# New places for all stages of a software-pipelined kernel, and the bias products moved to its prologue

## The chip, the cores and the metric

One core of a Trainium2 chip. The time is the device time of one execution, in microseconds (us). PE is TensorE, DVE VectorE, ACT ScalarE, POOL GpSimd, SP the engine that issues the transfers here.

## The reference, cut to what matters

x is 8 x 16 x 16 tokens of 64 channels. First comes a deformable convolution, then a mixture of experts of which two of eight are kept per token:

```python
xn = layernorm(x)                                    # over the channels
x_proj = xn @ w_in + b_in
x1 = gelu(layernorm(depthwise_conv3x3(xn)) * gamma + beta)
offset = x1 @ w_off + b_off                          # 8 groups x 9 taps x 2
mask = softmax(x1 @ w_mask + b_mask)                 # over the 9 taps
out = sum over taps of mask * bilinear_sample(x_proj, position + offset)
x = x + out @ w_out + b_out
z = layernorm(x)
w = the two largest of softmax(z @ Wr + br), divided by their sum
h_e = gelu((z * ln_g[e] + ln_b[e]) @ W1[e] + b1[e])
x = x + sum over e of w_e * (h_e @ W2[e] + b2[e])
```

ln_b[e] @ W1[e] + b1[e] does not depend on the tokens. The kernel computes it once, as eight products of 64 x 8 by 64 x 256 that add up in one PSUM bank (bias_product, line 1612), and puts it as two extra rows, high and low part, under the experts' first weights (bias_rows, line 925).

## The kernel before

The 2048 tokens are four chunks of 512 (CHUNKS), each of four tiles of 128. The program of every engine is a prologue, four bodies (j = 0 to 3) and a tail. Body j does three things side by side:

- The sampling of chunk j, in 36 steps (NP: four group pairs of nine taps). A step makes interpolation weights by two products (weights_t), ACT brings them to SBUF (weights_out), and a step and a half later PE multiplies them with the image (gather: 4 tiles x 3 products). Six tile results fill one of two PSUM banks; DVE multiplies a full bank with the column weights (weigh, 24 times a body). PE may start bank m only when bank m - 2 was weighed. After nine steps POOL adds the taps (tap_tree) and DVE adds the lanes in two halves (lane_sum).
- The preparation of chunk j + 1 ("a"): transposes of the normalised input (input_t), its low part (input_low), convolution (convolve, four), projection, the image's transposes (image_t, image_out), LayerNorm and Gelu (conv_norm, conv_t, conv_gelu), offsets, and on DVE positions, clamps, cells, rows, fractions, products (the last parts of the features), edges, hats, tap weights and column weights; features_t and table_out make the table for the steps of the next body.
- The experts for chunk j - 1 ("d"): samples_t, project_out, residual, inner_norm, experts_t, zn_low, router, route, 16 expert_in, 16 hidden (Gelu on ACT), four expert_out of two experts, outputs_out, outputs_t, outputs_in and, on POOL, combine.

In body 3 there is no next chunk. Its chunk is done in two halves of two tiles, so that it has 72 places with half as much work each, the experts for chunk 2 run beside it, and the experts of its own first half are begun (half_samples_t and the others). The tail does the experts of chunk 3.

What sets the order is a table for each engine and body (PE_FIRST to POOL_LAST, from line 62): for every stage the place at which the engine's program issues it. Places run from 0 to 35.5 in halves (0 to 71.5 in body 3). At a whole place n stands weights_t of step n, at n + 0.5 the gather of step n - 1; weighing m is issued at the place where its last step ends, after the stages of the same place. A place is an order within one engine's program, no time: where a stage waits for another engine, the engine's program stands at that place.

Products of zeros (keep_clock, line 1622) keep PE busy in waits; FILL holds their numbers in the prologue, "zeros" the places in bodies 0 and 3 where two are made. SP (line 500) loads all inputs, then waits for the two bias rows (line 521) and copies them with 16 transfers of 16 x 16 values into the weights' rows; PE waits for these before body 1 (line 1823).

## Time and profile before

| | |
|---|---|
| three executions | 310.0, 309.98, 307.35 us |
| median | 309.98 us |
| the profiled execution's own time | 309.92 us |
| its span, first to last instruction | 308.1 us |
| PE busy | 269.5 us (87%) |
| DVE busy | 238.4 us (77%) |
| ACT busy | 190.3 us (62%) |
| POOL busy | 120.6 us (39%) |
| mean clock granted to PE | 0.972 of 2.4 GHz |

A busy time counts a PE product with its way through the pipeline, so products that follow each other overlap; their cost is the distance of two starts. The windows further down divide the span by bodies: body 0 begins at 31.3 us with the first product of its step 0, body 1 at 89.2, body 2 at 158.2, body 3 at 222.5, and the last gather ends at 282.6.

### The profile page before, as it was taken

The page shows a single profiled execution, that of the slowest core. Times are in us where ns is not written, and L with a number is a line of the kernel's source. Part 1 is how long each engine was busy: PE and PEld are TensorE (multiplying, and loading weights), DVE is VectorE, ACT ScalarE, POOL GpSimd, SP SyncE. Part 2 cuts the span into 40 slices and gives each one's busy share as a digit, 9 for nine tenths or more (in the row PEclk, how much of TensorE's full clock was granted, in tenths as well). Part 3 has the DMA queues.
Part 4 walks back from the last instruction along what each step waited for, and adds up shares of the span by engine and source line. Part 5 has one row for each costly group of instructions (what it writes and reads, how often), then busy time and mean ns, then how long its engine had stood idle before and what let it go on. Part 6 is the DMA issues. An engine that isn't in the chain of part 4 may idle for free.

```text
span 308.1 us, 8247 instructions
## 1 busy us (share of the span) xinstructions
PE 269.5 (87%) x3312; PEld 178.5 (58%) x3312; DVE 238.4 (77%) x680; ACT 190.3 (62%) x351; POOL 120.6 (39%) x123
## 2 busy tenths in 40 slices
PE   6975999774897998899799999988978999989795
PEld 2552467542565766354477765535757788677462
DVE  6999868999977589995889589998757446189455
ACT  3786446573753397788365678775545685746363
POOL 6230132310750431405096605050575373648530
PEclk9998999999897899999999999997999999999999
DMA  5920000000000000000000000000000000000000
GB/s 149 291 54 0 2 3 3 3 0 0 2 2 0 2 4 3 2 0 2 0 2 20 2 3 0 2 0 2 3 17 2 2 3 2 9 2 2 10 2 17
DMA packets 7187, 4.83 MB, mean 16 GB/s; under 512 B 5089, under 2 KB 6830, under 8 KB 7086
## 3 DMA queue, kind: packets, MB, share of 16 engines
q1 hardware_dynamic: 7150, 4.31, 5.7%
q8 instruction: 26, 0.43, 0.6%
q14 instruction: 11, 0.09, 0.1%
HBM read 2.04 MB, written 0.52 MB: 8 GB/s over the span
## 4 chain that ended last, share of the span: by engine, by line
PE 43%; DVE 39%; POOL 10%; issue 4%; ACT 2%; DMA 1%; DVEq 0%; POOLq 0%; ACTq 0%
DVE prod L891 6%; DVE samp L906 4%; PE ga_ps L1579 4%; PE z_ps L1547 3%; PE z_ps L1549 3%; PE ga_ps L1581 3%; PE m_ps L1681 3%; PE ga_ps L1580 3%; PE z_ps L1561 3%; POOL prod L566 2%; PE m_ps L1648 2%; PE m_ps L1693 2%; PE m_ps L1664 2%; PE m_ps L1650 2%; PE m_ps L1471 2%
## 5 line engine op out<-in xcount | busy, mean ns | idle before, releaser
L1306 ACT ACTIVATE wk<-z_ps 128x512 int32<-128x512 f32 x108 | 64.6, 598 | 56.4 <-PE z_ps L1549 55.9
L1579 PE MATMUL ga_ps<-v_all,wk 128*128 128x80 f16 x576 | 79.3, 204 | 11.4 <-DVE prod L891 11.1
L891 DVE TENSOR_TENSOR prod<-ga_ps,wx 128x480 f32<-128x480 f32 x96 | 61.6, 650 | 27.6 <-PE ga_ps L1581 27.3
L566 POOL TENSOR_TENSOR prod<-prod 128x960 f32<-128x960 f32 (+1 forms) x20 | 36.5, 1825 | 113.5 <-DVE prod L891 113.5
L1579 PEld LDWEIGHTS ga_ps<-v_all,wk 128*128 128x128 f16 x576 | 57.7, 101 | 38.4 <-issue 17.3
L1580 PE MATMUL ga_ps<-v_all,wk 128*128 128x80 f16 x576 | 79.2, 204 | 0.0
L1581 PE MATMUL ga_ps<-v_all,wk 128*128 128x80 f16 x576 | 79.1, 204 | 0.0
L1580 PEld LDWEIGHTS ga_ps<-v_all,wk 128*128 128x128 f16 x576 | 58.2, 101 | 7.9 <-issue 1.1
L1581 PEld LDWEIGHTS ga_ps<-v_all,wk 128*128 128x128 f16 x576 | 58.4, 101 | 0.0
L1547 PE MATMUL z_ps<-tab,sel_hi 128*128 128x512 f16 x108 | 42.6, 394 | 0.5 <-ACT tab L1298 0.5
L1549 PE MATMUL z_ps<-tab,sel_lo 128*128 128x512 f16 x108 | 42.4, 393 | 0.0
L1337 ACT ACTIVATE h_all<-m_ps 128x512 f32<-128x512 f32 x64 | 36.9, 601 | 7.3 <-PE m_ps L1650 6.3
L1313 ACT ACTIVATE wk<-z_ps 128x512 int32<-128x512 f32 x36 | 21.5, 597 | 19.8 <-PE z_ps L1561 19.8
L906 DVE TENSOR_REDUCE samp<-prod 128x16 f32<-128x320 f32 x48 | 20.5, 476 | 2.4 <-POOL prod L568 1.8
L568 POOL TENSOR_TENSOR prod<-prod 128x320 f32<-128x320 f32 (+1 forms) x20 | 17.8, 892 | 1.6
L1561 PE MATMUL z_ps<-tab,sel_hi 128*128 128x256 f16 x72 | 17.7, 273 | 0.2 <-ACT tab L1298 0.2
L1561 PE MATMUL z_ps<-tab,sel_lo 128*128 128x256 f16 x72 | 17.6, 272 | 0.0
L1625 PE MATMUL ga_ps<-still 128*128 128x512 f16 x52 | 14.9, 428 | 3.0 <-DVE uloc L807 1.2
L567 POOL TENSOR_TENSOR prod<-prod 128x320 f32<-128x320 f32 (+1 forms) x20 | 15.6, 781 | 1.6
L1648 PE MATMUL m_ps<-zn_both,w_high 128*128 128x256 f16 x64 | 15.7, 274 | 0.2 <-ACT h_all L1337 0.2
L1650 PE MATMUL m_ps<-zn_high,w_low 97*128 97x256 f16 x64 | 15.7, 273 | 0.0
L1664 PE MATMUL m_ps<-h_all,w_s 128*64 128x512 f32 x64 | 15.5, 605 | 0.0
(279 smaller groups left out, 577.0 us busy)
## 6 DMA issues: line engine op xcount, KB each, us to landing
v_all<-still SPq DMA_DIRECT2D x1, 1440.0 KB, 10.7
h_all<-in_W SPq DMA_DIRECT2D x1, 512.0 KB
w_s<-in_W SPq DMA_DIRECT2D x1, 512.0 KB
x_tok<-in_x SPq DMA_DIRECT2D x1, 384.0 KB, 6.7
out_dram<-x_tok SPq DMA_DIRECT2D x6, 64.0 KB, 1.7
w_high<-w_high SPq DMA_DIRECT2D x1, 256.0 KB, 3.0
const<-in_table SPq DMA_DIRECT2D x1, 218.0 KB, 2.7
vec<-in_vectors SPq DMA_DIRECT2D x1, 132.5 KB
```

The lines of the kernel that those rows point to most:

```text
L566: then(pool.tensor_tensor(p[:, 0:3, :], p[:, 0:3, :], p[:, 3:6, :], ALU.add))
L891: dve.tensor_tensor(prod[q % 2][:].rearrange("p k n -> p (k n)")[:, f * PB * NV:(f + 1) * PB * NV] .rearrange("p (n c l) -> p n c l", n=PB ...
L906: ins = dve.tensor_reduce(samp[:, t, 2 * q:2 * q + 2, :], prod[q % 2][:, 5:K2, t * NV:(t + 1) * NV] .rearrange("p k (c g l) -> p g c k l", ...
L1306: act.activation(wk[n % WR][:], z_ps[use % 2][:], ACT.Relu, scale=HIGH_UNIT * FINE / Z_UNIT).then_inc(s_wk, 1)
L1337: act.activation(h_t[n % HR].rearrange("p a n -> p (a n)"), m_ps[n % 2], ACT.Gelu, scale=1.0 / (W1_SCALE * Z_SCALE)).then_inc(s_ht, 1)
L1547: pe.matmul(z_ps[use % 2][:], sel_hi[:, 2 * k:2 * k + 2, :].rearrange("p g m -> p (g m)"), tab[j % 2][:, q, :], start=True, stop=False)
L1549: pe.matmul(z_ps[use % 2][:], sel_lo[:, 2 * k:2 * k + 2, :].rearrange("p g m -> p (g m)"), tab[j % 2][:, q, :], start=False, stop=True).th ...
L1561: ins = pe.matmul(to, sel[:, 2 * k:2 * k + 2, :].rearrange("p g m -> p (g m)"), tab[LAST % 2][:, q, tokens_of(half)], start=(sel is sel_hi ...
L1579: pe.matmul(to, w_h, high, start=True, stop=False)
L1580: pe.matmul(to, w_h, low, start=False, stop=False)
L1581: ins = pe.matmul(to, w_l, step, start=False, stop=True)
L1648: pe.matmul(m_ps[n % 2][:, a * 2 * P:(a + 1) * 2 * P], w1_high[:, c0:c0 + P], zn_both[:, i * 2 * P:(i + 1) * 2 * P], start=True, stop=False)
```

## The change

All tables get new places. The stages of the preparation go some 2 to 12 places later in bodies 0 to 2, the expert stages some 5 to 10 places later; in body 3 the expert stages of chunk 2 go from places 11 to 48 to places 32 to 71.5, and those of the first half from 50 to 60.5 to 69 to 71.5. Two lines of the tables and what they became, of PE in body 1 and of DVE in body 0:

```diff
-PE_SECOND = {"input_t": 0, "convolve": [5, 5.5, 6, 10], "project": 4, "image_t": [11, 12], "conv_t": 14, "offsets": 15.5,
+PE_SECOND = {"input_t": 2.5, "convolve": [13.5, 15.5, 7, 7.5], "project": 12, "image_t": [17, 18.5], "conv_t": 22.5,
...
-             "zn_low": 17, "route": [18, 23, 25.5], "expert_weights": 26, "b2": 0, "bias_rows": 5, "router_parts": 31,
+             "zn_low": 17, "route": [18, 23, 25.5], "expert_weights": 26, "b2": 2.5, "bias_rows": 27, "router_parts": 8,
```

The eight bias products leave body 0 of PE (places 0 to 5.5). Four stand in the prologue after the convolutions, where FILL[3] goes from 13 products of zeros to 3, and four after the offsets, where FILL[4] goes from 7 to 0. They write the second gather bank instead of the second m bank; ACT copies the result to SBUF, DVE's bias_rows reads that copy, and PE's second gather bank waits for it once.

```diff
@@ -134,7 +132,7 @@
 
 
 
-FILL = [9, 2, 9, 13, 7, 6, 2]
+FILL = [9, 2, 9, 3, 0, 6, 2]
 
 FIRST = -(-6 * TP // PB)
 HALF_FIRST = -(-6 * TH // PB)
@@ -255,6 +253,7 @@
         b2_col = sb("b2_col", [P, E // 2])
         b1_in = sb("b1_in", [E, HID])
         b1_sum = sb("b1_sum", [E, HID])
+        lnb_w1 = sb("lnb_w1", [E, HID])
         b1_high = sb("b1_high", [E, HID], F16)
         b1_low = sb("b1_low", [E, HID], F16)
         lng_s = sb("lng_s", [C, E])
@@ -427,6 +426,7 @@
         s_still = sem("s_still")
         s_lngs = sem("s_lngs")
         s_lnb_ps = sem("s_lnb_ps")
+        s_lnb = sem("s_lnb")
         s_bias = sem("s_bias")
         s_w1h = sem("s_w1h")
         s_w1d = sem("s_w1d")
@@ -924,8 +924,9 @@
 
             def bias_rows():
 
-                dve.wait_ge(s_lnb_ps, 1)
-                link(dve.tensor_tensor(b1_sum[:], m_ps[1][0:E, 0:HID], b1_in[:], ALU.add))
+                dve.wait_ge(s_lnb, 1)
+                dve.wait_ge(s_wd, N_WD)
+                link(dve.tensor_tensor(b1_sum[:], lnb_w1[:], b1_in[:], ALU.add))
                 ins = dve.tensor_scalar(b1_high[:], b1_sum[:], W1_SCALE, None, ALU.mult)
                 ins.then_inc(s_bias, 1)
                 dve.wait_ge(s_bias, 1)
@@ -1337,6 +1338,11 @@
                 act.activation(h_t[n % HR].rearrange("p a n -> p (a n)"), m_ps[n % 2], ACT.Gelu,
                                scale=1.0 / (W1_SCALE * Z_SCALE)).then_inc(s_ht, 1)
 
+            def bias_product_out():
+
+                act.wait_ge(s_lnb_ps, 1)
+                act.copy(lnb_w1[:], ga_ps[1][0:E, 0:HID]).then_inc(s_lnb, 1)
+
             def high_w1():
 
                 act.wait_ge(s_wd, N_WD)
@@ -1444,6 +1450,7 @@
             ins.then_inc(s_sel, 1)
             for l in range(LOC):
                 distance(0, l)
+            bias_product_out()
             table_out(0, 0)
             tap_exp(0)
             table_out(0, 1)
@@ -1569,6 +1576,8 @@
                 for i, t in enumerate(tiles):
                     slot = n * len(tiles) + i
                     m, at = slot // PB, slot % PB
+                    if at == 0 and FILLS * j + m == 1:
+                        pe.wait_ge(s_lnb, 1)
                     if at == 0 and FILLS * j + m >= 2:
                         pe.wait_ge(s_ga_rd, FILLS * j + m - 1)
                     high, low, step = (v[:, 2 * j + t // 2, part, q, :, :, :].rearrange("p c g l -> p (c g l)")
@@ -1613,8 +1622,7 @@
 
                 if e == 0:
                     pe.wait_ge(s_wd, N_WD)
-                    pe.wait_ge(s_vd, 1)
-                ins = pe.matmul(m_ps[1][0:E, 0:HID], lnb_at(e), w1_raw[:, e * HID:(e + 1) * HID],
+                ins = pe.matmul(ga_ps[1][0:E, 0:HID], lnb_at(e), w1_raw[:, e * HID:(e + 1) * HID],
                                 start=(e == 0), stop=(e == E - 1))
                 if e == E - 1:
                     ins.then_inc(s_lnb_ps, 1)
@@ -1748,13 +1756,10 @@
                     if j == 0:
                         for at_zeros in at["zeros"]:
                             if n == at_zeros:
-                                pe.wait_ge(s_bias, 2)
+                                pe.wait_ge(s_vd, 1)
                                 keep_clock(m_ps[1], 2)
                         if n == at["b2"]:
                             columns_b2()
-                        for e in range(E):
-                            if n == at["bias_product"][e]:
-                                bias_product(e)
                     if has_a:
                         if n == at["input_t"]:
                             input_t(j + 1)
@@ -1802,12 +1807,16 @@
             for t in range(TP):
                 convolve(0, t)
             keep_clock(ga_ps[0][:], FILL[3])
+            for e in range(E // 2):
+                bias_product(e)
             pe.wait_ge(s_ident, 2)
             image_t(0, 0)
             conv_t(0)
             image_t(0, 1)
             pe.wait_ge(s_ones, 1)
             offsets(0)
+            for e in range(E // 2, E):
+                bias_product(e)
             keep_clock(ga_ps[0][:], FILL[4])
             pe.wait_ge(s_uloc, 1)
             keep_clock(ga_ps[0][:], FILL[5])

```

On PE, in the prologue, behind the last convolution (still is the tile of zeros, h_all holds the raw first weights, vec the experts' LayerNorm biases), before:

```order
L1493 MATMUL m_ps<-bias,ones 128x64
L1625 MATMUL ga_ps<-still 128x512 x13
L1514 MATMUL m_ps<-own_row,xq_left 64x96
L1515 MATMUL m_ps<-row_below,xq_left 64x32
L1514 MATMUL m_ps<-own_row,xq_left 64x96
```

and now:

```order
L1500 MATMUL m_ps<-bias,ones 128x64
L1633 MATMUL ga_ps<-still 128x512 x3
L1625 MATMUL ga_ps<-h_all,vec 8x256 x4
L1521 MATMUL m_ps<-own_row,xq_left 64x96
L1522 MATMUL m_ps<-row_below,xq_left 64x32
```

Four bias products stand between the remaining zeros and the image's transposes.

On DVE, in body 0, around the bias rows (b_sum, b_high, b_low; prod<-ga_ps is a weighing, samp<-prod a lane sum), before:

```order
L891 TENSOR_TENSOR prod<-ga_ps,wx 128x480
L928 TENSOR_TENSOR b_sum<-m_ps,b_in 8x256
L929 TENSOR_SCALAR b_high<-b_sum 8x256
L932 SCALAR_TENSOR_TENSOR b_low<-b_sum,b_high 8x256
L891 TENSOR_TENSOR prod<-ga_ps,wx 128x480
L740 SCALAR_TENSOR_TENSOR xq<-m_ps,image_bias,xq 64x256 x2
L744 COPY xq_left<-xq 128x2x16x3
L891 TENSOR_TENSOR prod<-ga_ps,wx 128x480 x2
L906 TENSOR_REDUCE samp<-prod 128x16 x4
L942 SCALAR_TENSOR_TENSOR w_low<-h_all,lng_s,w_high 64x256 x2
L891 TENSOR_TENSOR prod<-ga_ps,wx 128x480
```

and now, with the parts of the features that follow them (feat, fine, low, wf, shape, low_at, rest):

```order
L891 TENSOR_TENSOR prod<-ga_ps,wx 128x480 x2
L929 TENSOR_TENSOR b_sum<-lnb_w,b_in 8x256
L930 TENSOR_SCALAR b_high<-b_sum 8x256
L933 SCALAR_TENSOR_TENSOR b_low<-b_sum,b_high 8x256
L820 TENSOR_SCALAR feat<-frq 128x16x18
L822 SCALAR_TENSOR_TENSOR fine<-feat 128x288
L823 SCALAR_TENSOR_TENSOR low<-fr,feat 128x288
L825 SCALAR_TENSOR_TENSOR wf<-feat,fine 128x288
L891 TENSOR_TENSOR prod<-ga_ps,wx 128x480 x2
L830 TENSOR_SCALAR feat<-low 128x16x18
L831 TENSOR_TENSOR shape<-wf,csq 128x288
L833 SCALAR_TENSOR_TENSOR low_at<-feat 128x288
```

The three instructions moved from behind the third weighing to behind the eighteenth.

On PE, near the end of body 3, behind the transposes of the first half's normalised tokens (const,zn; the router is w_r_high and w_r_low, h_all,w_s an expert's second product, const,y_sb the outputs' transposes, ga_ps<-v_all,wk the gather, z_ps<-tab the weights of a step), before:

```order
L1469 MATMUL m_ps<-const,zn 64x128 x2
L1561 MATMUL z_ps<-tab,sel_hi 128x256
L1561 MATMUL z_ps<-tab,sel_lo 128x256
L1561 MATMUL z_ps<-tab,sel_hi 128x256
L1561 MATMUL z_ps<-tab,sel_lo 128x256
L1579 MATMUL ga_ps<-v_all,wk 128x80
L1580 MATMUL ga_ps<-v_all,wk 128x80
L1581 MATMUL ga_ps<-v_all,wk 128x80
L1579 MATMUL ga_ps<-v_all,wk 128x80
L1580 MATMUL ga_ps<-v_all,wk 128x80
L1581 MATMUL ga_ps<-v_all,wk 128x80
```

and now, where it is the last place of the body:

```order
L1588 MATMUL ga_ps<-v_all,wk 128x80
L1589 MATMUL ga_ps<-v_all,wk 128x80
L1590 MATMUL ga_ps<-v_all,wk 128x80
L1476 MATMUL m_ps<-const,zn 64x128 x2
L1613 MATMUL m_ps<-w_r_high,zn_both 128x8
L1614 MATMUL m_ps<-w_r_low,zn_both 128x8
L1613 MATMUL m_ps<-w_r_high,zn_both 128x8
L1614 MATMUL m_ps<-w_r_low,zn_both 128x8
L1689 MATMUL m_ps<-h_all,w_s 64x256 x8
L1701 MATMUL m_ps<-const,y_sb 128x128 x8
L1588 MATMUL ga_ps<-v_all,wk 128x80
L1589 MATMUL ga_ps<-v_all,wk 128x80
```

The router followed six steps after its transposes and now follows at once, and behind it stand the last expert products, the outputs' transposes and the last gathers.

## Rows read from the trace of the kernel before

**Rows 1.** Windows: busy time by engine; bodies 0 to 3.

```profile
31.30:89.20 57.90, 48.06 (x665) 30.56 (x664) 51.33 (x138) 32.41 (x55) 17.18 (x13) 0.97 0.01 2
89.20:158.20 69.00, 62.40 (x764) 39.58 (x762) 54.09 (x147) 45.24 (x80) 23.90 (x18) 0.95 0.01 2
158.20:222.50 64.30, 60.73 (x760) 38.71 (x758) 55.59 (x138) 43.75 (x79) 25.55 (x23) 0.97 0.02 4
222.50:282.60 60.10, 55.27 (x774) 45.03 (x775) 36.57 (x95) 35.11 (x67) 35.31 (x37) 1.00 0.02 5
```

**Rows 2.** Waits by engine, longest first.

```profile
PE z_ps L1539 <- DVE feat L843: 7.0, 2, 4.1
...
DVE prod L891 <- PE ga_ps L1581: 27.3, 23, 3.0
```

**Rows 3.** Timeline of PE: first product of two steps in a row.

```profile
52.02 0.38 PE L1547 MATMUL z_ps<-tab,sel_hi 128*128 128x512 f16 x1
...
52.88 0.38 PE L1547 MATMUL z_ps<-tab,sel_hi 128*128 128x512 f16 x1
```

**Rows 4.** Windows: start of body 0, places 3 to 6 of body 1, 70 to 80.

```profile
31.30:46.20 14.90, 14.90 (x195) 8.29 (x194) 11.32 (x31) 6.78 (x13) 3.91 (x3) 1.00 0.01 3
92.30:103.40 11.10, 9.01 (x99) 6.70 (x96) 6.42 (x22) 3.55 (x7) 2.50 (x2) 0.69 0.01 1
...
70.00:80.00 10.00, 5.25 (x55) 3.44 (x53) 8.95 (x24) 4.41 (x8) 1.49 (x1) 0.83 0.01 2
```

**Rows 5.** Timeline of PE: a bias product (two passes a row).

```profile
40.76 0.60 PE L1617 MATMUL m_ps<-h_all,vec 64*8 64x256 f32 x2
```

**Rows 6.** Timeline of PE and ACT in the prologue.

```profile
12.16 2.97 PE L1625 MATMUL ga_ps<-still 128*128 128x512 f16 x13
...
15.42 0.24 PE L1514 MATMUL m_ps<-own_row,xq_left 128*64 128x96 f16 x2 [0.29 <-DVE xq_left L744]
...
22.33 1.47 PE L1625 MATMUL ga_ps<-still 128*128 128x512 f16 x6 [1.17 <-DVE uloc L807]
...
12.79 3.30 ACT L1345 ACTIVATE w_high<-h_all,lng_s 64x256 f16<-64x256 f32 x8 [0.48 <-DMA b_in<-in_b]
```

**Rows 7.** Timeline of DVE and SP, and landings of b1's rows.

```profile
42.16 0.41 DVE L932 SCALAR_TENSOR_TENSOR b_low<-b_sum,b_high 8x256 f16<-8x256 f32 x1
...
48.25 5.76 SPq L524 DMA_DIRECT2D w_low<-b_low  x8
...
DMA to landing us min/median/max: 1.7/1.7/2.9
```

**Rows 8.** Timeline of DVE in body 0: stages counted behind the bias rows.

```profile
69.98 0.29 DVE L820 TENSOR_SCALAR feat<-frq 128x288 f16<-128x288 f32 x1
71.53 0.31 DVE L830 TENSOR_SCALAR feat<-low 128x288 f16<-128x288 f32 x1
74.54 0.65 DVE L891 TENSOR_TENSOR prod<-ga_ps,wx 128x480 f32<-128x480 f32 x1
76.22 0.45 DVE L862 TENSOR_REDUCE esum<-ex 128x32 f32<-128x288 f32 x1
77.78 0.65 DVE L891 TENSOR_TENSOR prod<-ga_ps,wx 128x480 f32<-128x480 f32 x1
```

**Rows 9.** The chain of waits, in order of time: a pair of experts out.

```profile
131.95 1.87 PE m_ps L1664 x8
```

**Rows 10.** Timeline of PE and ACT, end of body 3: transposes, router, copies.

```profile
274.43 0.38 PE L1469 MATMUL m_ps<-const,zn 128*64 128x128 f32 x2
...
276.51 0.18 PE L1604 MATMUL m_ps<-w_r_high,zn_both 128*128 128x8 f16 x1
...
266.80 1.56 ACT L1365 ACTIVATE y_sb<-m_ps,b_col 128x256 f32<-128x256 f32 x4
```

**Rows 11.** One line's instructions (ns min/median/max), and POOL beside the slow one.

```profile
L781 DVE TENSOR_SCALAR pyc<-py x4: 300/640/1317, 20.4 to 186.4; 128x288 f32<-128x288 f32 x4
...
58.72 2.22 POOL L566 TENSOR_TENSOR prod<-prod 128x960 f32<-128x960 f32 x1 [5.43 <-DVE prod L891]
```

More of the change, by code:

```diff
@@ L58 @@
 TINY = 2.0 ** -120
-PE_FIRST = {"input_t": 4, "convolve": [7, 8.5, 8.5, 9.5], "project": 6.5, "image_t": [10, 11.5], "conv_t": 14.5, "offsets":
-            15.5, "table": [24.5, 27], "samples_t": 24.5, "project_out": 8.5, "experts_t": 17.5, "router": 27, "expert_in":
-            [22, 35.5, 35.5, 35.5, 35.5, 35.5, 35.5, 35.5, 35.5, 35.5, 35.5, 35.5, 35.5, 35.5, 35.5, 35.5], "expert_out":
-            [17, 17.5, 20.5, 21, 21, 22.5, 25, 30], "outputs_t": [29.5, 30], "b2": 0, "bias_product": [0, 0, 1, 1, 3, 4, 4.5,
-            5.5], "zeros": [19, 22, 18.5]}
@@ L96 @@
-DVE_THIRD = {"input_stats": 0, "input_norm": 19.5, "input_low": 0, "conv_stats": 10, "project_low": 4.5, "conv_norm": 10,
-             "image_out": 12.5, "positions": [13.5, 14.5, 14], "rows": [18, 18, 19.5, 24], "edges": 18.5, "hats": 30,
-             "tap_weights": [29, 31], "lane_sum": [13, 17.5, 21, 23, 27.5, 29, 0, 0], "residual": 3, "inner_norm": 5,
-             "zn_low": 9, "route": [10.5, 15, 21], "expert_weights": 23.5, "b2": 25.5, "bias_rows": 5, "router_parts": 0,
+PE_FIRST = {"input_t": 6.5, "convolve": [10, 10.5, 10.5, 10.5], "project": 10, "image_t": [13, 15.5], "conv_t": 17,
+            "offsets": 18, "table": [34, 34], "samples_t": 24.5, "project_out": 8.5, "experts_t": 17.5, "router": 27,
+            "expert_in": [22, 35.5, 35.5, 35.5, 35.5, 35.5, 35.5, 35.5, 35.5, 35.5, 35.5, 35.5, 35.5, 35.5, 35.5, 35.5],
+            "expert_out": [17, 17.5, 20.5, 21, 21, 22.5, 25, 30], "outputs_t": [29.5, 30], "b2": 3.5, "zeros": [32, 34, 31]}
@@ new lines @@
+POOL_FIRST = {"tap_tree": [0.5, 13, 27.5, 29.5], "combine": [31, 32.5], "conv_rstd": 0, "inner_rstd": 4, "input_rstd": 0}
+PE_SECOND = {"input_t": 2.5, "convolve": [13.5, 15.5, 7, 7.5], "project": 12, "image_t": [17, 18.5], "conv_t": 22.5,
+             "offsets": 27, "table": [33.5, 35.5], "samples_t": 9, "project_out": 10, "experts_t": 15.5, "router": 17.5,
+             "expert_in": [19, 19, 19.5, 20, 22, 23, 24.5, 25, 28.5, 30, 31, 31, 31.5, 31.5, 32.5, 33], "expert_out": [29,
+             31, 33, 33.5], "outputs_t": [35, 35.5], "b2": 17.5}
@@ new lines @@
+PE_THIRD = {"input_t": 3, "convolve": [18, 17.5, 12.5, 18], "project": 8, "image_t": [15, 22], "conv_t": 25, "offsets": 26,
+            "table": [33.5, 35.5], "samples_t": 6.5, "project_out": 10, "experts_t": 16, "router": 19.5, "expert_in": [20.5,
+            21.5, 22, 25, 25.5, 26.5, 28.5, 29, 30, 30.5, 31, 31.5, 31.5, 32.5, 33, 33], "expert_out": [28, 31, 33, 33.5],
+            "outputs_t": [35, 35.5], "b2": 9.5}
+ACT_SECOND = {"pad_image": 4, "project_high": 12, "image_out": 17, "conv_gelu": 22, "tap_exp": 28, "distances": [31, 31, 31,
+              31.5, 33], "samples_out": 8.5, "zn_out": 15, "router_exp": 27.5, "hidden": [18, 18.5, 20, 21.5, 23, 23.5, 24.5,
+              25.5, 29, 29.5, 30, 30, 31, 31, 31.5, 32], "outputs_out": [30, 32.5, 33.5, 33.5]}
@@ new lines @@
+ACT_THIRD = {"pad_image": 3.5, "project_high": 10.5, "image_out": 15, "conv_gelu": 25, "tap_exp": 26.5, "distances": [30.5,
+             30.5, 31, 32, 32], "samples_out": 8, "zn_out": 16, "router_exp": 26.5, "hidden": [20, 23, 23, 26, 26, 28.5,
+             28.5, 29, 30, 31, 31, 31.5, 31.5, 31.5, 32, 32], "outputs_out": [29.5, 31, 33.5, 33.5]}
+DVE_SECOND = {"input_stats": 8, "input_norm": 22.5, "input_low": 2.5, "conv_stats": 18.5, "project_low": 12.5, "conv_norm":
+              20, "image_out": 16.5, "positions": [25.5, 27, 25.5], "rows": [27.5, 29.5, 30, 30.5], "edges": 27, "hats":
+              30.5, "tap_weights": [28, 34], "lane_sum": [20, 14.5, 21.5, 24, 34, 35.5, 5, 6], "residual": 8.5, "inner_norm":
+              12.5, "zn_low": 14.5, "route": [16, 20, 22.5], "expert_weights": 28, "b2": 8.5, "bias_rows": 21,
+              "router_parts": 14.5, "w1_low": [0.5, 7, 12, 13.5], "outputs_in": [35, 35]}
```

68 lines of the change are left out of this document (26 added, 42 removed).

## The prediction

> **What bounds the kernel now.** I read the windows first, one for each body of the loop [rows 1]; a row has the stretch, its length, the busy time of PE, of PE's weight loads, DVE, ACT and POOL with their instructions, and then the clock granted to PE, 1.00 being 2.4 GHz and 0.50 its other level of 1.2. The four bodies take 57.9, 69.0, 64.3 and 60.1 us, the prologue before them 31.3, the tail after them 25.5 of the span's 308.1. In body 0 DVE is the busier (51.3 us against PE's 48.1). In bodies 1 to 3 it is PE (62.4, 60.7 and 55.3 us), and the share of idle PE is 6.6, 3.6 and 4.8 us. So a new order can win back waits, and half-clock time, and nothing else: the arithmetic is the same but for the products of zeros.
>
> Then the waits by engine [rows 2]: PE waits 7.0 us for DVE's last feature, in two places, once 4.1; DVE in turn waits 27.3 us for PE. The two are tied: PE may be at most two banks (3 steps) ahead of the weighing. A step of bodies 0 to 2 costs PE 0.86 us (one selection product starts at 52.02, the next at 52.88 [rows 3]); the weighing is 0.65 us of DVE for each 1.5 steps, 1.29 us of PE. Each stretch of three steps thus takes the larger of the two engines' loads in it, and the places decide how well the loads match.
>
> Last the two worst matched stretches [rows 4]. From 31.3 to 46.2 body 0 does six steps (5.2 us of PE) in 14.9 us, PE never idle: eight bias products (0.5 us each [rows 5]), transposes, convolutions; DVE has 3.6 us idle there and is the bound of that body afterwards. From 92.3 to 103.4 body 1 does three steps in 11.1 us at a mean clock of 0.69; a quarter sum, its transposes and the output projection meet there, and PE ends it at half clock.
>
> **The sum, against the profiled execution's own 309.92 us** (span 308.1 and 1.8 around it; the median of the runs shown is 309.98, nearly the same).
>
> Prologue: 0. Ten zero products of 13 go, at 0.23 us each (2.97 us for 13 [rows 6]), 2.3 us, and four bias products of 0.5 come, 2.0. They now wait for all weights, and these had landed by 12.79 us, when ACT began on them [rows 6]. With 0.7 us of zeros after 12.16 PE is ready for them at 12.9, and done at about 15.0, ahead of the 15.42 at which the image transposes start on a DVE result. The second four take the place of seven zeros, and end at 21.7, before the 22.33 at which the next zeros wait for DVE [rows 6]. ACT's new copy of 8x256 comes after the distances, where ACT waits for PE's table transposes anyhow. If the weights landed 0.5 us later, the image transposes would be 0.5 us late: bounds 0 and +0.5.
>
> Body 0: -3.0. The bias products leave PE's full stretch: up to 4.0 us of PE, of which DVE can use at most its idle 3.6 us [rows 4]. DVE's own work is unchanged, so that is the most; the least is 0, if DVE meets other waits (the input's residue now waits on a chain PE, ACT, DVE from place 6 on). I take -3.0, near the row. The 4.1 us that PE stood for the last feature bring nothing by themselves: DVE was busy around it (8.95 of 10 us [rows 4]), and in the new order DVE has as much to do.
>
> Gate of body 1: +2.1. This is what the change adds. PE waits before body 1 for the 16 row transfers of b1; SP issues them after DVE's three instructions on the bias rows. Before, these ended at 42.57; the second eight issues ended at 54.01, and a transfer lands 1.7 us after its issue (at worst 2.9) [rows 7]: 13.1 us from DVE's end to the last landing, with 34 us to spare. Now the bias rows stand at place 27 of 35. Behind them DVE has up to its 22nd weighing: a third part of the features of 1.55 us, two weighings, the last part of 3.0, a quarter's half sum of 0.8, a weighing, tap weights of 1.55, a weighing [rows 8]: 7.2 + 2.2 = 9.4 us with weighings at 0.6 (0.65 each, overlapping a little). Thereupon PE needs only some 0.5 us more to reach body 1, so it stands 13.1 - 9.9 = 3.2 us. Its first gather there completes the 24th bank, which DVE would weigh at +11.7 otherwise (9.4, hats 0.9, a weighing 0.6, half a quarter's sum 0.8); with PE freed at 13.1 and 0.9 us for its first step it comes at about +14.0, 2.3 less some handover. DVE is the bound here, so I take the lateness on DVE, 2.1 us. Bounds: 0 if DVE loses 3 us to port or ACT waits in between, and 3.2 + 1.7 = 4.9 if PE's clock falls as well (a fall lasts about 3.4 us at half speed in this trace: 0.83 over ten us [rows 4], so 3.4 at 0.5).
>
> Opening of body 1: -5.2. Samples go from places 3 and 4 to 9 and 10, the convolutions behind them, the last quarter's sums from 1 to 5 and 6. The old stretch took 11.1 us [rows 4], its work at full clock is three steps (2.6), transposes 0.6, output projection 1.1, input projection 0.5, two convolutions 1.1: 5.9. This work is done later but without the meeting. Bounds: -6.5 (three steps and a transpose alone, 3.2 us, in place of 11.1, less 1.4 of what moves later into idle PE) and 0 (the chain meets another one at place 9); I stay at the row.
>
> Rest of bodies 1 and 2: +0.7. I added up each engine's stages for every three steps, at the old places and at the new, and took the larger load. The prices are start to start: a step 0.86 us of PE, an expert's half in 0.44, a pair of experts out 1.85 (eight products, 131.95 [rows 9]), four transposes 0.5, the offsets 1.5, a table 0.85, and on DVE a weighing 0.6, a clamp group 0.9, the parts of the features 0.8, 1.0, 1.5 and 3.0. For the old places these sums give 55.6, 66.8, 61.7 and 56.7 us, 240.8 in all, against 251.3 measured, the same order of the bodies and 4% short. Body 1 without the stretch above goes from 61.1 to 59.5, body 2 from 61.7 to 64.0. The loss is at places 27 to 30 of body 2, where rows, fractions, products, clamps and edges stand close (DVE 10.1 us, PE 5.3), then PE holds 17.7 us in the last six steps against 10.5 before. Bounds -3 and +5.
>
> Body 3: -1.5. PE needs 53.5 us of its 60.1 by the same sums. The expert work moves behind place 36, so the first half is gathers only, 0.43 us a step, where DVE has 0.2. It loses at the end: samples and projection of the first half now stand in one place (0.7 us wait), router behind its own transposes without cover: 274.43 to 276.51 [rows 10], 2.1 us less 0.4 of transposing, and the outputs' transposes behind the last expert product and two copies (0.8 us of the 1.56 [rows 10] and handover): 1.0. That is 3.4 of waits, with 1.7 for the rest, against 6.6 before. Bounds -4 and +4.
>
> Tail: 0. It holds the same work. POOL now has both combines before the last reciprocal root; by the same counting they are done 1 us before it is asked for. Bounds -1 and +2.
>
> Sum: -3.0 + 2.1 - 5.2 + 0.7 - 1.5 = -6.9, hence 303.0 us.
>
> A cost across all bodies is who runs beside POOL. The clamp of line 781 took 0.30 us at best and 1.32 at worst, which was at 59.8, when POOL's tree had started at 58.72 and runs 2.22 us [rows 11]. The Trainium skill, in SBUF — State Buffer, section SBUF: two separate sides, says that DVE in a two-port mode and GpSimd lock one pair of ports for a whole instruction, and the other fully blocks; the trace agrees by those two rows. By the rule every clamp that meets a tree costs 1.0 us more than one alone, and one meeting more or less than now in each of three bodies would move the sum by 3 us. From the rows alone the bounds are -1.0 (the one at 59.8 alone in future) and +3 (one such meeting more in each of bodies 0 to 2); I take 0, since trees and clamps both move.
>
> **Rivals.** (a) The gate does not bind, and the bodies match as well as the sums say: 303.0 - 2.1 - 2 = 298.9. For it: every wait above is a latency once, and hand sums count them in full. Against: the old bodies took 10.5 us more than such sums. Chance 0.2.
>
> (b) Nothing comes of it, 309: PE's busy 269.5 us stay, the openings win 6 us and the ends of bodies 1 and 2, now full, give it back. For: PE bounds these bodies in any order. Against: the 11.1 us stretch was waits and half clock, not work. Chance 0.14.
>
> (c) Slower, 313.4: the crowded ends. In places 27 to 36 of bodies 1 and 2 stand PE 23, DVE 21 and ACT 20 us, each waiting on the others by two-deep buffers: where they alternate in place of overlapping, each end loses what the old opening lost, 5.2 us, so +10.4 on 303.0. It decides from 6.9 us on. For: three engines near full. Against: the old places 24 to 36 of body 2 held as dense a PE. Chance 0.14.
>
> The forecast, 299 to 307, has 0.52. A measurement of this kernel can tell about 1%, 3.1 us, from no change. Faster by over 1% is a and most of the forecast, 0.7; within 1% 0.15; slower 0.15. The range leaves out 1 in 10 on each side: 296.5 to 311.
>
> **What would show it.** Right: body 1 starts near 84 us instead of 89.2, with a PE wait of about 3 us for DMA just before it and a bank weighed late; its places 3 to 6 take 3 to 4 us at full clock; body 2 no shorter than 63; router gap of 1.7 us near the end of body 3; tail 25. Wrong: PE without a DMA wait at body 1 (a), ACT and DVE each idle 4 us or more within the last nine steps of bodies 1 and 2 (c), or a clock under 0.9 in two or more of them.

## The result, and the profile after

The changed kernel takes 282.29 us (median of four, 280.76 to 284.77) against 309.99 in the same job, a ratio of 0.913 (0.905 to 0.922): 27.7 us less, where 6.9 were predicted, outside the range. The profiled execution took 282.16 us, its span 280.1. Windows of the bodies after, to be read against [rows 1]:

```profile
30.80:80.50 49.70, 43.70 (x650) 28.93 (x649) 48.29 (x140) 31.98 (x54) 17.44 (x13) 0.98 0.01 2
80.50:140.00 59.50, 59.48 (x758) 38.58 (x759) 50.30 (x143) 44.71 (x79) 21.50 (x17) 0.97 0.01 2
140.00:197.60 57.60, 57.50 (x760) 37.02 (x759) 49.71 (x139) 43.32 (x79) 24.27 (x22) 1.00 0.02 4
197.60:255.10 57.50, 54.02 (x776) 44.38 (x775) 37.27 (x95) 34.86 (x67) 36.70 (x39) 1.00 0.02 4
```

Body 0 lost 8.2 us, body 1 9.5, body 2 6.7, body 3 2.6, prologue and tail 0.5 each: 28.0, the difference of the spans. In bodies 1 and 2 PE is now busy without a pause (59.48 of 59.50, 57.50 of 57.60), and its busy time fell with its waits, from 60.73 to 57.50 in body 2, with 760 products before and after. DVE's fell as well, by 3.0, 3.8 and 5.9 us, though its work is nearly the same.

The waits, against [rows 2] (the first line is of the kernel before, of body 0 alone; the others are of the changed kernel):

```profile
PE z_ps L1539 <- DVE feat L843: 4.1, 1, 4.1
...
DVE prod L891 <- PE ga_ps L1590: 20.0, 20, 3.4
PE ga_ps L1588 <- DVE prod L891: 2.5, 3, 1.0
PE z_ps L1546 <- DVE feat L843: 2.3, 1, 2.3
```

Of the two feature waits before, 7.0 us in all, one of 4.1 stood in body 0, and it is gone; the other stands in the prologue in both kernels, 2.9 us before and 2.3 after. The gate before body 1 (timelines of SP and PE, against [rows 7]):

```profile
74.28 5.01 SPq L524 DMA_DIRECT2D w_low<-b_low  x8
...
80.53 0.52 PE L1554 MATMUL z_ps<-tab,sel_hi 128*128 128x512 f16 x1 [1.88 <-issue]
...
80.00:84.00 4.00, 3.48 (x29) 2.34 (x30) 2.06 (x3) 1.20 (x2) 2.81 (x3) 0.58 0.02 4
```

The last issue ends at 79.3, and PE stands 1.88 us for its landing. In the window from 80 to 84 us (third line) the granted clock is 0.58. The end of body 3, against [rows 10]:

```profile
248.91 0.38 PE L1476 MATMUL m_ps<-const,zn 128*64 128x128 f32 x2
250.49 0.18 PE L1613 MATMUL m_ps<-w_r_high,zn_both 128*128 128x8 f16 x1 [1.19 <-DVE zn_both L984]
253.59 0.66 PE L1701 MATMUL m_ps<-const,y_sb 128*128 128x128 f32 x4 [0.96 <-ACT y_sb L1371]
```

The pairs of experts out in body 2, beside which DVE's rows, fractions and products ran (timeline of PE):

```profile
183.09 1.94 PE L1672 MATMUL m_ps<-h_all,w_s 128*64 128x512 f32 x8
...
188.97 1.94 PE L1672 MATMUL m_ps<-h_all,w_s 128*64 128x512 f32 x8
...
191.82 1.94 PE L1672 MATMUL m_ps<-h_all,w_s 128*64 128x512 f32 x8
```

What had not been read before the change is this. Timeline of DVE and of POOL in body 2, first before, where the clamp of line 782 begins 0.05 us behind the first sum of one of POOL's trees and ends 0.16 us behind that sum's end:

```profile
186.58 2.33 DVE L782 TENSOR_SCALAR xa<-px 128x288 f32<-128x288 f32 x1
...
189.06 0.97 DVE L786 TENSOR_SCALAR xb<-xa 128x288 f32<-128x288 f32 x1
...
186.53 2.22 POOL L566 TENSOR_TENSOR prod<-prod 128x960 f32<-128x960 f32 x1 [10.01 <-DVE prod L891]
```

and after, where no tree runs beside it:

```profile
179.01 0.30 DVE L782 TENSOR_SCALAR xa<-px 128x288 f32<-128x288 f32 x1
179.23 0.30 DVE L784 TENSOR_SCALAR yr<-pyc 128x288 f32<-128x288 f32 x1
179.45 0.30 DVE L786 TENSOR_SCALAR xb<-xa 128x288 f32<-128x288 f32 x1
```

I took for every DVE instruction its duration less the shortest of the same form in any run, and added up what is over 0.12 us. Bodies 0 to 3 give 3.1, 4.0, 6.1 and 2.3 us before, 15.5 in all, and 0.9, 0.7, 0.0 and 2.3 after, 3.9 in all. Every instruction in this sum overlaps one of POOL. Weighings, which read PSUM, stay at 0.63 to 0.66 us each. The lane sums stay as they are too, though their input and output are in SBUF (before, ns min/median/max):

```profile
L906 DVE TENSOR_REDUCE samp<-prod x48: 466/476/487, 48.0 to 225.6; 128x16 f32<-128x320 f32 x48
```

### The profile page after: what moved, and what is told of

The parts are those of the page before. It is cut to its first block, busy times and chain, and to the rows that moved or that the text cites. A ratio compares the mean times of both kernels' runs of the same rounds, so it can differ in the third digit from the quotient of the medians.

```text
span 280.1 us, 8214 instructions
## 1 busy us (share of the span) xinstructions
PE 259.0 (92%) x3295; PEld 172.8 (62%) x3295; DVE 226.5 (81%) x680; ACT 189.0 (67%) x352; POOL 118.6 (42%) x123
## 3 DMA queue, kind: packets, MB, share of 16 engines
HBM read 2.04 MB, written 0.52 MB: 9 GB/s over the span
## 4 chain that ended last, share of the span: by engine, by line
PE 68%; DVE 21%; POOL 4%; issue 4%; ACT 1%; DMA 1%; DVEq 0%; POOLq 0%; ACTq 0%
PE ga_ps L1588 7%; PE z_ps L1554 7%; PE z_ps L1556 6%; PE ga_ps L1590 6%; PE ga_ps L1589 6%; PE m_ps L1672 5%; PE z_ps L1568 5%; DVE prod L891 4%; PE m_ps L1689 3%; PE m_ps L1650 3%; PE m_ps L1651 2%; PE m_ps L1656 2%; PE m_ps L1658 2%; PE m_ps L1701 2%; PE m_ps L1478 2%
## 5 line engine op out<-in xcount | busy, mean ns | idle before, releaser
L1307 ACT ACTIVATE wk<-z_ps 128x512 int32<-128x512 f32 x108 | 64.3, 600 | 36.7 <-PE z_ps L1556 36.3
L1588 PE MATMUL ga_ps<-v_all,wk 128*128 128x80 f16 x576 | 77.7, 203 | 3.7 <-DVE prod L891 2.5
L1589 PE MATMUL ga_ps<-v_all,wk 128*128 128x80 f16 x576 | 77.6, 203 | 0.0
L1590 PE MATMUL ga_ps<-v_all,wk 128*128 128x80 f16 x576 | 77.5, 203 | 0.0
L1588 PEld LDWEIGHTS ga_ps<-v_all,wk 128*128 128x128 f16 x576 | 57.1, 100 | 31.3 <-ACT wk L1307 12.3
L566 POOL TENSOR_TENSOR prod<-prod 128x960 f32<-128x960 f32 (+1 forms) x20 | 38.6, 1930 | 87.4 <-DVE prod L891 87.4
L1589 PEld LDWEIGHTS ga_ps<-v_all,wk 128*128 128x128 f16 x576 | 57.6, 100 | 7.2 <-issue 0.5
L1590 PEld LDWEIGHTS ga_ps<-v_all,wk 128*128 128x128 f16 x576 | 57.8, 100 | 0.0
L1568 PE MATMUL z_ps<-tab,sel_hi 128*128 128x256 f16 x72 | 17.7, 274 | 0.0
L1568 PE MATMUL z_ps<-tab,sel_lo 128*128 128x256 f16 x72 | 17.7, 272 | 0.0
L567 POOL TENSOR_TENSOR prod<-prod 128x320 f32<-128x320 f32 (+1 forms) x20 | 14.8, 742 | 1.6
L1672 PE MATMUL m_ps<-h_all,w_s 128*64 128x512 f32 x64 | 15.5, 605 | 0.0
L568 POOL TENSOR_TENSOR prod<-prod 128x320 f32<-128x320 f32 (+1 forms) x20 | 14.7, 736 | 1.6
L1633 PE MATMUL ga_ps<-still 128*128 128x512 f16 x35 | 12.7, 513 | 1.9 <-POOL still L594 1.1
```

The lines of the kernel that those rows point to most:

```text
L566: then(pool.tensor_tensor(p[:, 0:3, :], p[:, 0:3, :], p[:, 3:6, :], ALU.add))
L1307: act.activation(wk[n % WR][:], z_ps[use % 2][:], ACT.Relu, scale=HIGH_UNIT * FINE / Z_UNIT).then_inc(s_wk, 1)
L1568: ins = pe.matmul(to, sel[:, 2 * k:2 * k + 2, :].rearrange("p g m -> p (g m)"), tab[LAST % 2][:, q, tokens_of(half)], start=(sel is sel_hi ...
L1588: pe.matmul(to, w_h, high, start=True, stop=False)
L1589: pe.matmul(to, w_h, low, start=False, stop=False)
L1590: ins = pe.matmul(to, w_l, step, start=False, stop=True)
```

## The experiments

Body lengths are those of the profiled execution, from one body's first weights product to the next one's. The runs were timed in several jobs. The kernel before had 309.99 us in the job of the changed kernel and 307.9 to 308.5 in the others, so a difference of less than 2 us between two medians is read from the body lengths.

**The two parts alone.** bias_only has the old places with the bias products in the prologue; places_only has the new places, with the bias products and the products of zeros where they were before. Of bias_only, the first of its tables against the changed kernel's:

```diff
-PE_FIRST = {"input_t": 6.5, "convolve": [10, 10.5, 10.5, 10.5], "project": 10,
+PE_FIRST = {"input_t": 4, "convolve": [7, 8.5, 8.5, 9.5], "project": 6.5,
...
```

> The old places of all stages, with the bias products in the prologue as in the changed kernel. If the new places did the work, 305 to 308 us: body 0 loses up to 3.6 us of PE time that kept DVE waiting, nothing else moves. If the moved products did a good part of it (a PE freed early in body 0 shifts all that follows), 300 or less, and the stretch from 92 to 103 us at half clock is gone.

> The new places of all stages, with the eight bias products and the products of zeros where they were before. If the new places did the work, 284 to 287 us: the changed kernel's 282.3 and the 4 us of PE that come back into body 0, as far as they aren't hidden. If the moved products did a good part of it, 292 or more.

bias_only: 308.05 us, ratio 0.999 (0.996 to 1.003). places_only: 288.27, 0.935 (0.929 to 0.940). The bias products' move is worth nothing at the old places and 6.0 us at the new ones, all in body 0 (56.1 to 49.7, where PE's wait at the gate is 2.5 in the one and 1.9 in the other). Waits of DVE in body 0, of the kernel before and of places_only:

```profile
DVE prod L891 <- PE ga_ps L1581: 0.7, 2, 0.4
...
DVE prod L849 <- PE ga_ps L1539: 4.4, 5, 1.7
```

At the old places DVE hardly waits for PE in body 0, so PE's freed time serves nobody: in bias_only the body is still 57.2 us, DVE is busy 51.87 of them, and its longest waits are for POOL. At the new places DVE would wait 4.4 us for PE with the bias products there, and its lengthened instructions would be 2.4 us in place of 0.9.

bias_only shows one thing more. Its body 2 has the same program as before and takes 62.7 us in place of 64.3; the granted clock is 1.00 there in place of 0.97. So about 1.6 us of what body 2 lost are half clock, which the same order of body 2 has in one kernel's execution and not in the other's.

**The gate.** gate_early puts the bias rows back to the start of body 0.

```diff
-"bias_rows": 27,
+"bias_rows": 3,
```

> The changed kernel with DVE's bias rows at place 3 in place of 27, so that their 16 transfers have landed long before body 1. If the gate costs what it looks like (1.88 us of PE wait before body 1, put down to issue), that wait is gone and the time is 280 to 281. If the wait is another's, or DVE is so far behind that PE would stand anyway, it stays at 282.3 within 0.5.

278.95 us (278.91 to 279.04), 0.905 (0.900 to 0.909): the wait is gone, 3.3 us are won (3.1 by the spans of the profiled executions), more than was expected, and this version beats both kernels. Body 0 is 47.4, body 1 58.1 at full clock (59.5 in the changed kernel), bodies 2 and 3 unchanged. Windows of bodies 0 and 1:

```profile
31.40:78.80 47.40, 42.89 (x651) 28.79 (x650) 46.26 (x136) 31.59 (x55) 15.74 (x13) 1.00 0.01 2
78.80:136.90 58.10, 57.89 (x762) 37.43 (x759) 52.45 (x147) 45.15 (x80) 24.58 (x17) 1.00 0.01 2
```

**One body at its old places.** In the changed kernel, all tables of body 1 (old_body1), all of body 2 (old_body2), and of body 1 the opening alone (old_opening, two cuts of its edit):

```diff
-"samples_t": 9, "project_out": 10,
+"samples_t": 3, "project_out": 4,
...
-"lane_sum": [20, 14.5, 21.5, 24, 34, 35.5, 5, 6], "residual": 8.5,
+"lane_sum": [20, 14.5, 21.5, 24, 34, 35.5, 1, 1], "residual": 4,
```

> The changed kernel with the old places in body 1 alone (all four engines). If each body's gain is its own, body 1 takes some 69 us again in place of 59.5 and the time is 290 to 293. If a body's loss comes from what its neighbours leave over (the quarter sum and the samples at its opening, at half clock), the old places cost less here, 287 or under, since body 0 now leaves no backlog.

> The changed kernel with the old places of body 2 alone. Theory A (old places cost waits between neighbouring steps of a chain, which the new ones put behind other work): body 2 goes from 57.6 back to about 64.3, with the bodies beside it unchanged, so 289.0 (+6.7), and the waits for DVE's last feature come back in it. The prediction's own sums had the old body 2 at 61.7 and the new one at 64.0: by them this kernel would be 2.3 us faster, 280.0. Rival E (a body's length is set by what its neighbours leave over): +2 to +4 only.

> The changed kernel with the opening of body 1 at its old places: the last quarter's sums at place 1 in place of 5 and 6, the samples' transposes at 3 in place of 9, output projection at 4 in place of 10, their copies likewise; the rest of the body stays new. The prediction's term for this stretch was 5.2 us, its bounds 0 and 6.5. Putting back all of body 1 has cost 7.1 us in body 1. Theory A (the opening is the larger part of it): body 1 goes from 59.5 to about 64.5, time 287.3. Rival F (the opening is a wait that half clock made long, while in the new order the convolutions and projection are away from it): +2, 284.3. Rival G (nothing, the waits move): within 0.7 of 282.3.

old_body1: 289.47, body 1 59.5 to 66.6, DVE's lengthened instructions in it 0.7 to 4.0 us. old_opening: 285.37, body 1 63.6, so 4.1 of these 7.1 are the opening; its wait is the old one, at a mean clock of 0.95 over the body:

```profile
86.23 0.72 PE L1438 MATMUL m_ps<-const,samp 128*128 128x128 f32 x4 [2.08 <-DVE samp L866]
```

old_body2: 286.68, body 2 57.6 to 63.5, lengthened instructions 0.0 to 6.2. The prediction's sums would have had it 2.3 us shorter. Window of its body 2:

```profile
138.70:202.20 63.50, 59.23 (x760) 37.63 (x758) 56.36 (x140) 43.96 (x79) 26.11 (x24) 1.00 0.02 4
```

**More work for one engine.** dve_more and dve_early add four DVE products (at places 27 to 30, and 4 to 7, of body 2), dve_little two; pe_more and pe_body0 make the four convolutions of body 2 or 0 twice. dve_more and pe_more stand on the changed kernel, the others on gate_early.

```diff
+                        if j == 2 and n in (27, 28, 29, 30):
+                            some = wx[0][:].rearrange("p n t l -> p (n t l)")[:, 0:480]
+                            dve.tensor_tensor(spare[:], some, some, ALU.mult)
...
-                for k in range(K2):
+                for _ in range(2 if a == 3 else 1):
+                    for k in range(K2):
```

> The changed kernel with four more DVE products of 128x480 fp32 into a spare tile, one at each of places 27 to 30 of body 2, where the prediction found DVE the crowded engine (10.1 us of DVE against 5.3 us of PE). Nothing reads them. Each should take about 0.5 us, near a weighing, 2.1 us in all. Theory A (PE alone bounds bodies 1 and 2 in the new order, DVE has slack everywhere but in body 0): the time stays at 282.3 within 0.7, body 2 stays at 57.6, and PE's idle gaps in it stay near none. Rival B (the prediction's sum: each three places take the larger engine's load): body 2 becomes 59.7 and the time 284.4. Rival C (DVE's burst is just covered, with 1 us to spare): between, +1, with a PE wait for a bank at places 30 to 32.

> The changed kernel with the four convolutions of body 2 (19 products each, 0.029 us apart in the trace) made twice, 76 more products, 2.2 us of PE at places 12 to 18 of body 2. Theory A (PE bounds body 2 without a pause): the time rises by all of it, 282.3 to 284.5, body 2 57.6 to 59.8. Rival B (each stretch takes the larger load, and behind this one DVE's burst at places 27 to 30 is the larger): DVE keeps running meanwhile, so the burst starts further ahead of PE, and part of the 2.2 is given back: +0 to +1.1. Rival D (PE's busy time is not its demand, short pauses are hidden in the busy time of pipelined products): also under 2.2.

> The kernel with the early bias rows (278.95), with four more DVE products of 0.65 us (2.6 us, read by nobody) at places 4 to 7 of body 2. At places 27 to 30 the same 2.6 us made bodies 2 and 3 1.7 us longer. Theory (PE runs two banks ahead, so DVE's idle 2.3 us of this stretch and the banks take it up): body 2 57.6 to 57.9, +0.3. Rival (the larger load of each three places: PE 3.1 and 3.6, DVE 3.2 and 1.2 there, so 3.2 would become 5.8): +1.5 to +2.6. If so then DVE is a bound everywhere in body 2 by nearly as much as PE.

> The kernel with the early bias rows (278.95), with two more DVE products of 0.65 us (1.3 us) at places 4 and 5 of body 2. Four of them at places 4 to 7 (2.6 us) have cost 2.0 in that body. Theory J (a margin: PE begins a bank 1.0 us after the weighing that frees it, in this stretch, and DVE waits 1.2 us for the next bank; what exceeds the margin costs): +0.0 to +0.4. Rival K (in proportion, as if DVE were the bound there): +1.0, as 2.0 of 2.6.

> The kernel with the early bias rows (278.95), with the four convolutions of body 0 made twice, 2.2 us more of PE at places 10 and 10.5. In body 0 DVE is busy 46.3 of 47.4 us and PE 42.9. Theory (DVE alone bounds body 0): body 0 47.4 to 47.9 at most, +0.5. Rival (both bind in turn, as in body 2, PE's work in one place delays the bank that DVE needs next): +1.5 to +2.2. The bias products are 4.0 us of PE in that body, and leaving them there has cost 6.0 (288.3 against 282.3): only by the rival could they.

pe_more: 283.81, body 2 59.7, +2.1 of 2.2 (the medians, of two jobs, give 1.5). dve_more: 284.08, four products of 0.65 us; body 2 58.7 and body 3 58.2, so +1.8 of 2.6. dve_early: 281.05, body 2 +2.0, but the four took 4.9 us, since the first met POOL's combine and the last a tree:

```profile
L1102 DVE TENSOR_TENSOR spare<-wx x4: 639/772/2670, 142.5 to 147.1; 128x480 f32<-128x480 f32 x4
...
146.68 2.56 POOL L527 TENSOR_TENSOR prod<-prod 128x960 f32<-128x960 f32 x1 [1.57 <-DVE prod L852]
```

dve_little: 279.38, +0.4 for 1.5 us: a margin, as theory J has it, and no proportion. pe_body0: 282.86, body 0 51.2, +3.8 for 2.2 us of PE. Against my theory PE's work counts there too, and more than once: DVE waited 2.2 us for PE, and by its lateness met POOL's tree with the input's normalisation, 0.43 us where alone:

```profile
56.79 2.32 DVE L669 TENSOR_TENSOR xn<-xn,x_rstd 128x256 f32<-128x256 f32 x1
```

So PE bounds body 2, DVE has a margin of about 1 us there (2.6 less 1.8 in dve_more, 1.5 less 0.4 in dve_little), and in body 0 both bind in turn.

**Moving work between bodies.** weights_back runs DVE's column weights at place 33.5 of body 0. lows_later moves the low parts of w1 to body 1, the waits for them to the first expert product, and three stages at body 3's end. Both on gate_early.

```diff
-"tap_weights": [31.5, 35.5]
+"tap_weights": [31.5, 33.5]
```

> The kernel with the early bias rows (278.95), with DVE's column weights of the next chunk (two halves of 1.7 us together) at place 33.5 of body 0 in place of 35.5. At 35.5 they run after the body's last weighings, beside the first products of body 1. Theory (body 0 is DVE's, body 1 is PE's, so the new places win by carrying 1.7 us of DVE over the boundary): body 0 47.4 to 49.1 at most, body 1 58.1 unchanged since PE is the bound there: +1 to +1.7 in all. Rival (they only fill a wait for PE at the boundary, and the first weighing of body 1 waits for them wherever they stand): within 0.5.

> The kernel with the early bias rows (278.95), and two more edits. (1) DVE's eight subtractions that make the low part of w1 (0.47 us each, 3.5 us in all) go from places 3.5 to 8 of body 0 to places 0.5 to 13.5 of body 1, and PE's wait for them and for the row transfers from the start of body 1 to its first expert product (place 19). Theory A (DVE bounds body 0, PE body 1, DVE having 6.1 us idle in body 1): body 0 47.4 to 44.5, body 1 58.1 to 58.6. Rival (in body 1 DVE is nearly as full as PE, and the crossing waits give it back): body 1 +2 or more, nothing won. (2) At the end of body 3 the first half's sample transposes go half a place earlier, its transposes for the router and the seventh expert product to place 71, so that this product stands between transposes and router: the router's wait 1.19 becomes 0.3, body 3 57.5 to 56.6; if the wait only moves to the next link, 57.5. In all 275.5 by theory, 278.9 by the rivals.

weights_back: 283.40, +4.5, all in body 1. Timelines of DVE (one tile) and POOL at the boundary:

```profile
L839 DVE TENSOR_TENSOR wx<-dl,mask x1: 3554/3554/3554, 79.1 to 79.1; 128x1440 f32<-128x1440 f32 x1
...
78.30 2.81 POOL L526 TENSOR_TENSOR prod<-prod 128x960 f32<-128x960 f32 x1 [9.08 <-DVE prod L851]
81.19 2.16 POOL L527 TENSOR_TENSOR prod<-prod 128x320 f32<-128x320 f32 x1
```

The tree was there in gate_early too, where this product began at 80.86, near the end of POOL's first sum, took 1.78 us, and POOL's second sum beside it 2.17 for 0.87. Two places earlier the product begins at 79.07 and stands through the rest of the first sum: 3.55 us for 1.66 alone, with POOL's second sum as before. PE stood 3.1 us for the weighing behind, and its granted clock was 0.53 for the next 3.5 us. lows_later: 283.92, +5.0, where 3.4 less were expected. Body 0 is 48.9, not 44.5 (DVE waits 2.5 us more and lengthens by 1.6 more), body 1 62.1, where the first four of the eight subtractions take 0.97 to 1.88 us for 0.47. Body 3 fell by 0.9 as expected, and the tail grew by 0.6.

**Half of body 2.** old_prep and old_prep2 (on gate_early) have body 2's preparation at the old places and its experts at the new. The edit that makes old_prep2 of old_prep, one root on POOL:

```diff
-"inner_rstd": 2.5
+"inner_rstd": 7.5
```

> The kernel with the early bias rows (278.95), and in body 2 the old places for everything that prepares the next chunk (input, convolutions, image, offsets, positions, rows, features, tables, weights, clamps, trees), while samples, router and experts of the chunk before keep their new places. All of body 2 at old places has cost 5.9 us in it. Theory A1 (each step's chain through PE, ACT and DVE needs several places between its parts, in both halves): the preparation is about half of the loss, body 2 57.6 to 60.5. Rival H (the experts' places are the loss, since the preparation is spread in both tables): under 1 us. Rival I (all of it: the waits for the last feature were the preparation's): +5 to 6. Old preparation beside new experts may also crowd less than either, -0.5 at most, since PE's own work is 57.5.

> As old_prep, but POOL's root of the residual's variance goes to place 7.5, behind the root of the convolution's (place 7), in place of 2.5 ahead of it and of a tree. In old_prep body 2 took 81.4 us, with 11.1 us in which POOL waited for the residual's variance, and 5.6 us in which DVE waited for the root behind it. Theory L (this crossing in POOL's order made most of the loss): body 2 about 63 to 66. Rival M (the old preparation itself does not fit the new experts' places on PE and DVE): 75 or more.

300.84 and 296.23: body 2 takes 81.4 and 74.2 us, far outside all that was expected of old_prep. The crossing on POOL was 7.2 of the 23.8 us; the rest fits rival M, that the halves do not fit each other, and no run takes it apart. The old body 2 as a whole costs 6. The losses of single stages don't add up to that of a table.

**Trees cut short.** The last three cut POOL's trees to 4 of 320 columns and leave the other columns' taps unsummed, so they compute something else and serve for timing alone: in the old body 2 (on gate_early), in all bodies before, and in all of gate_early.

```diff
-                then(pool.tensor_tensor(p[:, 0:3, :], p[:, 0:3, :], p[:, 3:6, :], ALU.add))
+                then(pool.tensor_tensor(p[:, 0:3, 0:4], p[:, 0:3, 0:4], p[:, 3:6, 0:4], ALU.add))
...
```

> The kernel with the early bias rows (278.95), with the old places of body 2 and with POOL's four trees of that body cut to 4 of their 320 columns (the other columns' taps are left unsummed). The old body 2 took 63.5 us, the new one 57.6, and 6.2 against 0.2 us of it are DVE instructions lengthened, all but 1.0 of that beside a tree. Theory P (old and new body 2 differ by whom a tree of POOL meets): body 2 takes 57.5 to 59. Rival Q (they differ by the waits between the steps of a chain; DVE's longer instructions stand in these waits): 62 or more.

> The kernel before, with all of POOL's trees cut to 4 of 320 columns (the other columns' taps are left unsummed). Lengthened DVE instructions are 15.4 us in its four bodies, about 12 of them beside a tree, and DVE waits 2.7 us for trees. Theory P: 308.3 becomes 293 to 297, bodies 54.5, 65, 58.5 and 59. Rival Q: no more than the waits for trees, 305 to 306.

> The kernel with the early bias rows (278.95), with all of POOL's trees cut in the same way. It has 5.2 us of lengthened DVE instructions, half of them beside a tree. Theory P: 276 to 279, bodies 46.5, 57.9, 57.6 and 57. Then the new places are worth some 17 us beyond the trees, in body 0 by the bias products (6) and in body 1 by its opening (4), the rest by waits. Rival Q: the same here, within 1 us of 278.95; what tells them apart is how far before_short_trees comes towards this one.

Old body 2: 61.3 us, DVE 51.19 busy in it for 56.36: 2.2 of the 5.9 us to the new body 2 are the trees', 3.7 are not. Both theories fall as sole cause. Before: 300.34, 0.970 (0.961 to 0.980), 7.6 us less; gate_early: 276.74, 0.897 (0.892 to 0.902), 2.2 less. The lengthened instructions fall from 15.5 to 1.0 us in the one and from 4.9 to 0.0 in the other, so the trees cause them. Windows of bodies 0 to 2 of the kernel before with short trees:

```profile
31.40:91.00 59.60, 52.17 (x667) 31.73 (x666) 48.30 (x139) 32.22 (x55) 5.45 (x13) 0.89 0.01 2
91.00:154.10 63.10, 59.16 (x763) 37.34 (x760) 50.33 (x147) 45.16 (x80) 8.39 (x19) 1.00 0.01 2
154.10:214.90 60.80, 58.79 (x760) 37.60 (x757) 50.51 (x138) 43.74 (x78) 12.70 (x23) 1.00 0.02 4
```

The 7.6 us are not the trees' company alone. Against [rows 1] the granted clock rose from 0.95 and 0.97 to 1.00 in bodies 1 and 2, which lost 5.9 and 3.4 us, and fell from 0.97 to 0.89 in body 0, which took 1.6 us longer. Only body 2 can be compared at full clock on both sides, at the old places: 62.7 us in bias_only and 60.9 here, and 63.5 (old_body2) and 61.3 behind a body 1 at the new places, so the trees cost about 2 us there. 5.4 us, the difference of 7.6 and 2.2, is thus a rough figure for all bodies.

## Why the prediction was wrong

The direction was right (0.7 for faster); the size was a quarter of the real one. By its steps:

- **Prologue and tail, 0 each**: 0.5 less each. The bias products fitted as worked out, ahead of the waits that follow [rows 6]; timeline of PE:

```profile
12.89 1.89 PE L1625 MATMUL ga_ps<-h_all,vec 64*8 64x256 f32 x8
...
15.41 0.24 PE L1521 MATMUL m_ps<-own_row,xq_left 128*64 128x96 f16 x2 [0.63 <-DVE xq_left L744]
```

- **Body 0, -3.0, and the gate, +2.1**: together -0.9 predicted, -8.2 measured. The gate's mechanism is shown: PE stood 1.88 us for the row transfers (3.2 expected), taking it away won 3.3, of which 1.4 in body 1, by its clock: old_body2, which has the wait and not the fall, has 58.2 there too. What failed is "DVE can use at most its idle 3.6 us" with "DVE's own work is unchanged". I counted idle time in the first 15 us; over the body it is 6.6, and 1.4 after. Of the 6.6 only 0.7 was a wait for PE, so the bias products alone could not win it (bias_only); the new places did. And DVE's busy time was no constant: it fell 3.0 us, 1.7 by one column weighting that now runs behind the boundary, 3.1 by two clamps, the hats and a copy that no longer meet a tree, less 1.0 for new meetings and 0.8 of stages that now fall inside the window.
- **Opening of body 1, -5.2**: 4.1 by old_opening.
- **Rest of bodies 1 and 2, +0.7**: -12.1 (-5.4 and -6.7). This is the worst step, and two parts of it failed. First the rule "Each stretch of three steps thus takes the larger of the two engines' loads in it". PE may be two banks ahead of DVE: when DVE began the clamps of its place 27, at 178.80, PE was past its place 28 (the pair at 176.35) and on its way to 31 (the pair at 183.09). In body 2 DVE's burst lasted from 178.8 to 192.4, and in that time PE did three pairs of experts (at 183.1, 189.0 and 191.8, the rows in the first section) and never waited: the two crowds that I added, 10.1 and 17.7 us, ran side by side. Body 2 takes PE's own work, 57.5, not 64.0. That the sums came within 4% of the old bodies was an accident: body 2 is 3.7 us longer at the old places even with short trees and full clock, which I take for handovers that the new places have spread, and the second part and half clock are on top.
- **Port, 0, bounds -1.0 and +3**: [rows 11] showed the effect, and the Trainium skill (SBUF — State Buffer, "SBUF: two separate sides") names instructions with two SBUF inputs beside the two-port ones. The trace agrees for elementwise instructions: xn, with two SBUF inputs, took 2.32 us beside a tree and 0.43 alone. I priced one line, at 1.0 us for each meeting, where one costs what is left of POOL's sum, 0.67 to 2.04 us for the clamps before. All lines together had 15.5 us in the four bodies, and 11.6 of it went; in time that is some 5 us by the short trees, with half clock mixed in. The term had to be a sum over all DVE instructions of duration less shortest duration, which the trace before gives.
- **The gate's sum**: the stages behind the bias rows come to 6.9 + 2.4 = 9.3 us as listed, not 7.2 + 2.2, which changes nothing.
- **Body 3, -1.5**: -2.6, with the waits named: router 1.19 (1.7 expected), outputs' transposes 0.96 (1.0), projection 0.47 (0.7). Its tables alone were not tried.

Reading PE's busy share as demand lies under all this. The sentence "the share of idle PE is 6.6, 3.6 and 4.8 us" took PE's 60.73 us in body 2 for work, but the same 760 products are busy 57.50 now, and were busy 59.23 at the old places at full clock (old_body2). So 1.5 us were half clock, and 1.7 went with the new order; I take them for short waits hidden inside overlapping products.

Of the rivals (a), 298.9, was nearest in its number and had its condition wrong, since the gate did bind. Of the signs, body 1 did begin earlier (80.5, where 84 was expected) behind a wait for the transfers, and the router's wait and the tail were as expected; "body 2 no shorter than 63" and a full clock at the opening of body 1 were wrong.

What stays open: of 27.7 us, some 5.4 go with the trees, 4.1 with the opening, 6.0 with the bias products at the new places, and these overlap. The other 12, body 3's 2.6 among them, no single run isolates. Handovers are my reading of most of it; half clock is a rival for a part: before, the bodies 1 and 2 had 0.95 and 0.97 of the clock, after 0.97 and 1.00, and in body 2 this was 1.6 us.
